# A field-pair tower with 32x64 instead of 32x128 weight tiles, a re-ordered opening, and the dense layers ahead of the sums

## The reference

```python
# ids (2048, 40), dense_ctx (2048, 16), 40 tables of (1000..125000, 32), all fp32
e = jnp.stack([tbl_0[ids[:, 0]], ..., tbl_39[ids[:, 39]]], axis=1)      # (2048, 40, 32)
iidx, jidx = jnp.triu_indices(40, k=1)                                  # 780 pairs of fields
z = jnp.einsum('bpd,pde,bpe->bp', e[:, iidx, :], bilinear, e[:, jidx, :])
h = jnp.concatenate([z, dense_ctx], axis=1)                             # (2048, 796)
h = jnp.maximum(h @ W_top1 + b_top1, 0.0)                               # 512
h = jnp.maximum(h @ W_top2 + b_top2, 0.0)                               # 256
return h @ W_top3
```

## Time and profile before

| | us |
|---|---|
| profiled execution, its own time | 700.91 |
| its span in the trace | 699.1 |
| median of 3 runs | 701.48 |
| opening, up to the first multiply | 35.80 |
| block 0, its 25 steps | 80.00 |
| block 4, its 25 steps | 79.99 |
| block 6, its 25 steps | 82.00 |
| last step and tail | 25.33 |

### The profile page before, as it was taken

How to read it: one execution, slowest core, us unless ns; L and a number is a source line. 1 busy time by engine, 2 the same in 40 slices (tenths; PEclk the granted TensorE clock), 3 DMA queues, 4 the chain that set the end, 5 groups by cost and what they waited for, 6 DMA issues and landing times.

```text
span 699.1 us, 25209 instructions
## 1 busy us (share of the span) xinstructions
PE 662.1 (95%) x11496; PEld 413.8 (59%) x11496; DVE 550.6 (79%) x630; ACT 140.3 (20%) x350; POOL 463.0 (66%) x494
## 2 busy tenths in 40 slices
PE   1769989999999999999999999999999999999998
PEld 0645655566666666656655656565665656565656
DVE  5788889887898787878888787888878787678860
ACT  5411202112221202220220112211131112310002
POOL 6777777777777777777777777777777777700000
PEclk9999999999999999999999999999999999999999
DMA  6480102111120100200112000210101100000000
GB/s 201 133 294 16 16 15 51 25 16 15 16 61 16 16 15 16 61 15 16 16 20 57 16 15 16 61 16 15 16 16 16 16 15 16 16 4 2 3 1 1
DMA packets 23500, 23.89 MB, mean 34 GB/s; under 512 B 10917, under 2 KB 20705, under 8 KB 23265
## 3 DMA queue, kind: packets, MB, share of 16 engines
q0 software_dynamic: 15360, 7.90, 7.3%
q1 hardware_dynamic: 7418, 13.80, 5.9%
q10 hardware_dynamic: 616, 0.58, 0.3%
HBM read 22.18 MB, written 0.06 MB: 32 GB/s over the span
## 4 chain that ended last, share of the span: by engine, by line
PE 88%; DVE 6%; ACT 2%; issue 2%; DMA 1%; SPq 0%; ACTq 0%; DVEq 0%
PE Y L531 26%; PE ZL L558 24%; PE ZL L583 16%; PE H L509 8%; PE Y L539 6%; PE H L495 5%; DVE prod L760 4%; DVE one L746 2%; ACT xcols L668 1%; PE Y L592 1%; PE Y L601 1%; DVE prod L766 1%; DMA idx<-ids 1%; PE H L592 0%; DMA tab<-tbl 0%
## 5 line engine op out<-in xcount | busy, mean ns | idle before, releaser
L469 POOL DMA_INDIRECT rows<-tbl,idx x480 | 461.5, 962 | 148.1 <-issue 145.4
L760 DVE TENSOR_TENSOR prod<-Y,xcols 128x1024 f32<-128x1024 f32 x296 | 348.6, 1218 | 72.7 <-PE Y L531 72.4
L531 PE MATMUL Y<-xcols,mats 32*128 32x256 f32 x2880 | 207.7, 401 | 12.1 <-DVE prod L760 5.1
L558 PE MATMUL ZL<-prod,sel 128*32 128x256 f32 x3200 | 217.5, 383 | 0.9 <-ACT z L675 0.2
L531 PEld LDWEIGHTS Y<-xcols,mats 32*128 32x128 f32 x2880 | 132.5, 184 | 91.9 <-issue 74.2
L766 DVE TENSOR_TENSOR prod<-Y,xcols 128x1024 f32<-128x1024 f32 x104 | 122.8, 1219 | 46.0 <-PE Y L531 29.7
L668 ACT ACTIVATE xcols<-H 32x256 f32<-32x256 f32 (+3 forms) x223 | 83.8, 376 | 322.1 <-PE H L495 213.2
L558 PEld LDWEIGHTS ZL<-prod,sel 128*32 128x32 f32 x3200 | 93.2, 110 | 70.2 <-issue 26.8
L583 PE MATMUL ZL<-z,w_sb 128*32 128x256 f32 x1568 | 105.9, 379 | 0.0
L746 DVE TENSOR_SCALAR one<-idb,count 125x1024 bf16<-125x1024 f16 (+1 forms) x200 | 83.0, 450 | 0.0
L583 PEld LDWEIGHTS ZL<-z,w_sb 128*32 128x32 f32 x1568 | 51.7, 110 | 33.3
(11 more groups left out here) (30 smaller groups left out, 74.0 us busy)
## 6 DMA issues: line engine op xcount, KB each, us to landing
rows<-tbl,idx POOLq DMA_INDIRECT x480, 2.4
idb<-ids_turned SPq DMA_DIRECT2D x8, 768.0 KB
w_sb<-w SPq DMA_DIRECT2D x1, 1792.0 KB
mats<-m_wide SPq DMA_DIRECT2D x1, 1152.0 KB, 8.8
mats<-m_wide SPq DMA_DIRECT2D x1, 960.0 KB, 10.7
tab<-tbl SPq DMA_DIRECT2D x8, 112.0 KB
mats<-m_wide SPq DMA_DIRECT2D x1, 768.0 KB, 4.8
w_sb<-w SPq DMA_DIRECT2D x1, 512.0 KB
```

Source lines behind the costliest of these rows:

```text
L469: pool.indirect_dma_start(out=rows[:, slot, t, D * q:D * (q + 1)], out_offset=None, in_=tables[f], in_offset=bass.IndirectOffsetOnAxis(ap= ...
L531: last = pe.matmul(Y[:, bank, cols], mats[D * r:D * (r + 1), unit_cols(u)], xcols[D * r:D * (r + 1), n % 2, a, :], start=True, stop=True, ...
L558: last = pe.matmul(Z[D * q:D * (q + 1), :], sel[:, GF * (SPAN - 1 - o):GF * (SPAN - 1 - o) + 32], prod[:, (2 * s + q // 2) % PROD, q % 2, ...
L760: dve.tensor_tensor(prod[:, half, :, :].rearrange("p b (u c) -> p (b u) c", c=BLK), Y[:, pair:pair + 2, :].rearrange("p b (u c) -> p (b u) ...
```

## The change

- Every unit is done in 32x64 tiles: per plain slot eight matmuls, columns 0 to 63 for the four quarters and then columns 64 to 127. A diagonal slot, now the upper part of one group's unit and the lower part of another's, also takes eight matmuls of the same form. L539 goes.
- The diagonal's products need a group whose partitions 0 to 63 are of one group and 64 to 127 of another: ACT makes five such mixed groups a block (`mix`, two copies each). In step 24 DVE has four instructions of 128x512 for two of 128x1024.
- `mlp` stands in front of `add_up`, but for the first step of a tile.
- Opening: all ids are turned at once; DVE, not ACT, saves those of blocks 1 to 7; each item of `HEAD` has a Y bank of its own; look-up 2 of block 0 goes from `HEAD` to steps 4 and 5; SP loads the third tables behind the first two pieces of `mats`; the last two casts and the last rest come later.
- Other hot waves and another order of groups. Blocks 4 to 7 look up waves 0 and 1 (before: 0 and 2). `HOT_RING` is 16 for 12. The planner of one-hots now counts PE's and DVE's work instead of spacing them evenly before their use.

```diff
-HOT = [(20, 21, 18, 23), (16, 13, 26, 11), (36, 33, 30, 15)]
+HOT = [(20, 21, 18, 23), (16, 25, 30, 15), (36, 33, 38, 11)]
...
-ORDER = [5, 4, 3, 2, 6, 7, 8, 9, 0, 1]
+ORDER = [5, 4, 7, 6, 3, 2, 8, 9, 0, 1]
...
-HOT_RING = 12
+HOT_RING = 16
...
-HEAD = [("turn", 0, 0), ("turn", 0, 1), ("hot", 0, 0), ("hot", 0, 1), ("turn", 0, 2), ("hot", 0, 2)]
-
-LANDED, PER_STEP = 14, 2.4
+
+HEAD = [("turn", 0, 0), ("turn", 0, 1), ("hot", 0, 0), ("turn", 0, 2), ("hot", 0, 1)]
+
+LANDED, PER_STEP = 12, 2.0
...
+UNITS_SUMS, LAYER, MODE, TURNED, PLACE = 197, 43, 11, 46, 33
+PRODUCTS, ONE_HOT, LATE = 238, 44, 20
...
-    at, pos = [0] * len(used), float(NB * NS)
-    for v in reversed(range(len(used))):
-        pos = min(used[v] - 2, pos - 0.9)
-        at[v] = -1 if used[v] < 0 else max(0, int(pos))
...
+    for s in range(NB * NS):
+        behind = max(behind, 0) + PRODUCTS - tensor_work(s)
+        while v < len(used) and (v < HOT_RING or used[v - HOT_RING] <= s):
+            if behind + ONE_HOT > LATE and used[v] > s + 1:
+                break
+            behind += ONE_HOT
+            at[v] = s
+            v += 1
...
-            load_tables(sp, 2)
+            sp.wait_ge(s_rest_ids, 1)
+            sp.dma_start(ids_turned[1:NB].rearrange("n j c -> j n c"),
+                         idt[:, BLK:BATCH].rearrange("j (n c) -> j n c", c=BLK)).then_inc(s_idd, DMA)
             load_mats(0)
             load_mats(1)
...
+            load_tables(sp, 2)
...
-                    if len(SLOTS[k]) == 1:
-                        u = SLOTS[k][0]
-                        a = UNITS[u][1]
+                    for c in range(2):
                         for r in range(GF):
-                            bank = 2 * ((2 * s + r // 2) % 3) + r % 2
-                            last = pe.matmul(Y[:, bank, cols], mats[D * r:D * (r + 1), unit_cols(u)],
-                                             xcols[D * r:D * (r + 1), n % 2, a, :], start=True, stop=True,
+                            u = SLOTS[k][1 if on_diagonal(k) and r > 2 * c else 0]
+                            b = bank_of(k, r)
+                            bank = 2 * ((2 * s + b // 2) % 3) + b % 2
+                            last = pe.matmul(Y[2 * D * c:2 * D * (c + 1), bank, cols],
+                                             mats[D * r:D * (r + 1), u * P + 2 * D * c:u * P + 2 * D * (c + 1)],
+                                             xcols[D * r:D * (r + 1), n % 2, UNITS[u][1], :], start=True, stop=True,
                                              skip_group_check=True)
-                    else:
-                        for h, u in enumerate(SLOTS[k]):
-                            G = UNITS[u][0]
-                            for r in range(2):
-                                bank = 2 * ((2 * s + h) % 3) + r
-                                last = pe.matmul(Y[:, bank, cols], mats[2 * D * r:2 * D * (r + 1), unit_cols(u)],
-                                                 xcols[2 * D * r:2 * D * (r + 1), n % 2, G, :], start=True, stop=True,
-                                                 skip_group_check=True)
...
                     for what in ITEMS[n * NS + w]:
                         fill(*what)
+                    if pn > 0 and pw % TILE > 0:
+                        mlp(pn - 1, *mlp_part(pw))
                     if pn >= 0:
                         add_up(pn, pw)
-                        if pn > 0:
-                            mlp(pn - 1, *mlp_part(pw))
+                    if pn > 0 and pw % TILE == 0:
+                        mlp(pn - 1, *mlp_part(pw))
...
+            def mix(n, k):
+                A, B = [UNITS[u][0] for u in SLOTS[k]]
+                act.wait_ge(s_free, mix_after(n, k) + 1)
+                act.activation(xcols[0:2 * D, n % 2, MIXED[k], :], xcols[0:2 * D, n % 2, B, :], ACT.Copy)
+                act.activation(xcols[2 * D:P, n % 2, MIXED[k], :], xcols[2 * D:P, n % 2, A, :], ACT.Copy).then_inc(s_mix, 1)
...
+            def save_ids():
+                dve.wait_ge(s_idt, 2)
+                for m in range(BT, MT, GF):
+                    bank, width = 1 + (m - BT) // GF, (min(m + GF, MT) - m) * P
+                    last = dve.tensor_copy(idt[:, m * P:m * P + width], Y[0:len(HOT_FIELDS), bank, 0:width])
+                last.then_inc(s_rest_ids, 1)
```

186 lines of the change are left out of this document (108 added, 78 removed).

## The result

| | before | after |
|---|---|---|
| median, us (range) | 701.52 (701.09 to 702.34) | 693.08 (692.29 to 694.74) |
| ratio, 95% interval | | 0.988 (0.986 to 0.990) |
| profiled execution, its span | 700.91, 699.1 | 694.74, 692.9 |
| opening, up to the first multiply | 35.80 | 38.70 |
| block 0 | 80.00 | 84.29 |

Faster by 1.2%, which is 8.4 us where 27.8 were forecast. By the profiled executions 21.6 us are missing. The first multiply of block 1 starts at 122.99, forecast 111.1: 11.9 us are lost ahead of it. The other 9.8 (all parts are rounded) are lost behind it, where 23.1 were forecast and 13.3 came.

What follows compares the result with a forecast made beforehand. PE, busy 95% of the span, was taken as the bound, with DVE the floor in the lightest steps and block 0. 16.5 + 4.9 + 1.3 + 1.9 + 0.5 + 4.7 - 2.0 = 27.8 us saved gave 673.7, range 665 to 687.

Steps and rivals of the forecast that it cites:

- The step that failed first: Opening: 12th gather and turn timing put the first multiply at about 28.2 instead of 35.80; with block 0, 4.7 us gained.
- Diagonal units: Blocks 1 to 7: diagonal multiplies as short as plain ones, 0.86 a full step, 0.63 the mixed one; 16.5 us saved.
- Rivals 2, 4 and 5: Multiplies: same-row loads queue, 684, chance 0.12; PE can't feed eight tiles, 714, 0.06; row-group rule shows loads, 706, 0.03.
- The seam: Steps 24 and 0 between blocks: ACT's mixed groups cost nothing, or 0.2 if ACT delayed one save of a tile.
- double turn: Block 6, step 24: two turns through bank H become one turn alone in its step, saving 1.9 us.
- The weight load: Multiplies of blocks 1 to 7: shorter 64-column loads save 0.03 each, 4.9 us, bounds +9 and -5; lightest steps gain too.
- Dense layers in front: Steps with dense layers: PE gets work while DVE ends its second half; 1.3 us saved, bounds 0 and 3.
- block 1's lumps: Block 1: one-hots made in lumps just before use make look-ups wait in six places; 2 us lost, bounds 0 and 4.
- Gathers: POOL's gathers: number 480 is out at 610, as now; no wait, and 25 us are left.
- Rival 3: Opening gives nothing, since block 0 is DVE's and DVE has more to do early; 678, chance 0.14.
- The bound "0 and 8": Opening and block 0: the gain, put at 4.7 us, lies between 0 and 8 us.
- rivals 1 to 3: Full weight-load gain and free lumps, 668, chance 0.16; same-row loads queue, 684, 0.12; opening gives nothing, 678, 0.14.

Runs made afterwards that it cites:

- e3: Against the changed kernel: the dense layers' matmuls put back behind the sums in every step; 693.33 us, ratio 0.989.
- f2: Against the changed kernel: plain slots back in 32x128 tiles, diagonal ones kept in 32x64; 694.62 us, ratio 0.992.
- e2: Against the changed kernel: the planner's two numbers set back to 14 and 2.4, so turns for the next block stand earlier; 688.79 us, ratio 0.983.
- f3: Against the changed kernel: last two pieces of mats, second ids and dense weights held until the turn of step 0 is copied; 691.58 us, ratio 0.987.
- e1: Against the changed kernel: mats from the third piece on, second ids and dense weights held until turn 2 is copied; 693.61 us, ratio 0.989.
- h1: Against the changed kernel: DVE makes eight opening one-hots, the next eight only after turn 2; 1231.81 us, ratio 1.019, in a run whose kernel before took 1208 to 1210.
- f4: Against the changed kernel: the edits of e2 and e4, the hold of f3, and ten block 0 one-hots moved before the first products; 683.05 us, ratio 0.975.
- e4: Against the changed kernel: ACT makes the mixed groups at the end of its step, behind the tile copies; 690.75 us, ratio 0.985.
- e6: The same kernel as f3, against the changed kernel, in another run; ratio 1.023, where the kernel before took 1208 to 1210 us.

## Why the prediction was wrong

**The step that failed first** is "the 12th is issued at 20.06 and a turn starts some 3.5 us behind its last gather". It took both from a trace in which neither the sixteen one-hots in a row nor the big loads lay there. I had listed both as moved, counted the one-hots on DVE alone, and never asked what SP's queue would issue once the ids no longer kept it waiting. The first multiply is 10.5 us late (in e3, f2 and e2, with the same instructions up to it, 9.4, 8.2 and 6.0), and the 10.5 has three parts:

| | forecast | after | f3 | e1 |
|---|---|---|---|---|
| 12th gather issued | 20.06 | 24.97 | 22.97 | 23.39 |
| from there to turn 2 | 3.44 | 6.48 | 3.04 | 3.17 |
| from turn 2 to the first multiply | 4.7 | 7.25 | 6.65 | 7.36 |
| first multiply | 28.2 | 38.70 | 32.66 | 33.92 |

- *The issue, 4.9.* Shown for the greater part: the one-hots hold it. In h1, where eight are made and not sixteen, the 12th gather is out at 20.55: the held gather and the one behind it take 1.18 and 0.94 there, in after 3.66 and 1.66, which is 3.2 of the 4.9. In the kernel before, rests stood between the one-hots in fours, and no gather of its opening took over 1.60. Gathers 5 and 6, which took 2.00 and 2.33 beside the id copies and rests on DVE, are 0.9 of it; in e3, f2 and h1 only the 7th is so long, 2.33. The remainder is the start of the first gather, some 0.3, and what h1 is still behind the forecast, 0.5. The Trainium skill has such a hold under "SBUF — State Buffer", SBUF: two separate sides: while DVE runs in a mode with two ports, POOL can't write the descriptors of its DMAs. The trace agrees in kind: a held gather ends 0.12 us behind DVE's last one-hot. It adds that the gather waited for the whole row of short instructions to end, not for one; that the one-hots run in such a mode, no row here shows.
- *The landing, 3.0.* Shown by e1 and f3, with f4: with the loads away it is 3.17, 3.04 and 3.07, with them 5.97 to 6.88 in six kernels (6.48 in after). The hold takes mats, ids and weights together, so which of them it is stays open. It isn't a free gain: whoever holds them has a later turn pay (turn 3 in e1, turn 4 in f4).
- *PE, 2.5.* Look-up 1 takes 4.66 for the 2.80 of the earlier trace rows, at a granted clock of 0.59 for 1.00. That is the clock's two levels (1.2 and 2.4 GHz) mixed: its rounds of four instructions stand 0.21 us apart, and 0.11 only at the end, where the kernel before has 0.11 throughout. Before, PE was busy most of the time up to it; after, it stood idle for 8.38. In e1 and f3, idle for 4.62 and 3.96, the look-ups took 4.78 and 4.14, so a shorter idle alone doesn't bring the clock back. The earlier trace rows had a look-up of 5.06 beside the one of 2.80, with its rounds 0.21 apart although the granted clock of its row reads 1.00; the forecast took the quick one without a reason. This part is read from traces, not isolated.

**From the first products on, block 0 was right.** The chain was to take 86.7 - 29.4 = 57.3 to the products of step 15; it took 97.46 - 40.08 = 57.4. That it is so close is in part luck: up to the products of step 6 it took 23.8 for 24.6, from there on 33.6 for 32.7. But the forecast that DVE has little slack there held, and for that reason the late start counted in full: in f3, with the first multiply 6.0 earlier, block 1 starts 6.1 earlier. Of the 11.9 missing at block 1, 10.5 are the first multiply; the rest are the last steps, among them step 24 at 3.35.

**Blocks 1 to 7.** Sums over these blocks, by kind of step:

| | forecast | measured | |
|---|---|---|---|
| steps 3 and 15 | -12.5 | -11.4 | right: two more turns stand there, 0.9 |
| steps 24 of blocks 1 to 6 | -5.9 | -2.7 | wrong |
| steps 0 | -0.2 | +2.8 | wrong |
| last step 24 | -0.7 | -0.7 | right |
| the other steps | -3.8 | -1.3 | mis-sized |

- *Diagonal units*: right. Steps of the same content went from 3.79 to 2.91, 0.88, against 0.86 + 0.03. Rivals 2, 4 and 5 fall. The row-group rule of the Trainium skill ("TensorE: Matmul & The Clock Gate", Part 3) would have each round show its loads; four rounds of eight tiles and a change of form in 1.05 leave no room for that.
- *The seam*: the second step that failed, and the larger share of what blocks 1 to 7 lack (6.2 of 9.8). "The mixed groups are ten copies a block on ACT ... Cost nothing", and the double turn's 1.9 and the 0.63 of step 24 counted as if nothing else would be late. In step 24 there is again a turn, whose four copies end after the multiply could start, and of the mixed step's 0.63 nothing is left over six blocks. ACT's busy share of 20% was the wrong view: what counts is the order of its queue in 3 us around the seam. e4 and e2 undo it, one by 3.0 us in steps 0, the other by 6.3 in both kinds, less 2.7 elsewhere. Shown.
- *The weight load*: the size was off. 0.03 a multiply came in steps with much work (2.94 to 2.91), and in the two halves that I had put: the second round starts 0.27 behind the first for 0.32, and the next group 0.35 behind the last round for 0.32. In the lightest steps the loop through DVE got longer instead: 2.59 for the 2.57 of the earlier trace rows. I had let them gain too. 4.9 was forecast (175 x 0.03 is 5.3, so the sum had it 0.4 too low), f2 measures 1.0, or 2.5 with steps 24.
- *Dense layers in front*: worth 0.0 by e3, not 1.3. Waits like that of the earlier trace rows went, but with the one-hots' places: they are as rare in e3. One new wait came in step 13, 3.14 or 3.15 in six blocks, where the copy of `h` is late by the three copies ahead of it; it is there in e3 too.
- *Block 6's double turn* went as forecast, and *block 1's lumps* cost about the forecast 2: steps 20 and 21 take 4.87 and 4.79 there, 4.10 in block 2.
- *Gathers*: the last one goes out at 616.6, forecast 610, with no wait at the end.

Rival 3 named the opening but gave it nothing; it cost 7.2. Its sign, products 15 of block 0 not before 89, came, at 97.46, and beyond what it meant: no rival had a loss there. The bound "0 and 8" for opening and block 0 excluded one without a reason. With a loss of 7 allowed there, beside the bounds of rivals 1 to 3, the range could have reached the result.

## What to carry to other kernels

When an edit takes instructions out of a queue, ask of every queue what now runs earlier, and lay those transfers and bursts beside the waits that the forecast shortens. A gather's time of issue, its landing and PE's clock all hang on what lies beside them, so a row of the kernel before gives them only while that stays. Look also for the odd long row among many equal ones: the gather of 2.19 among those of 0.94 was in the trace before, beside just the kind of row on DVE that the change put into the opening. And where a cheap engine feeds two others, read the order of its queue around each seam, not its busy share.

## What the runs showed of the hardware

- Eight 32x64 tiles of fp32 run at once (eight starts within 0.05 us), 32 instructions in 1.05 us with a change of form, with weight loads of 131 ns hidden.
- One gather on POOL was held from within a burst of bf16 one-hots on DVE until 0.12 us behind its end: 3.66 and 7.86 with sixteen and 32, where it took 1.18 with eight. The gathers behind it, once DVE was free, went on at 0.94. It wasn't always the same gather (2.07 in e2, 2.46 in e6), and one row of 26, most of half the size, held none.
- Beside full DMA engines a turn starts 6.0 to 6.9 us after its last gather's issue, in six kernels; 3.0 to 3.2 without, in three.
- The same instructions brought the first multiply at 34.21 to 38.70 in four executions of the opening.
